# Graph attention and a mixture of experts on one core: the V projection moved into the batch before, four of 32 transposed copies moved to VectorE, and the second K projection moved to slot 7

## The reference, cut to what matters

```
x: (16, 512, 256) float32,  adj: (16, 512, 512) int32,  8 heads of 32

def gnn(x, adj):                       # x is the layer-normed input
    q, k, v = x @ Wq.T, x @ Wk.T, x @ Wv.T        # split in 8 heads
    s    = where(adj != 0, q @ k^T / sqrt(32), -inf)
    attn = softmax(s)
    c    = attn @ v
    gate = sigmoid(concat(c, x) @ Wg.T + bg)
    return gate * x + (1 - gate) * c

x = x + gnn(layernorm(x), adj)
x = x + ffn(layernorm(x))              # 8 experts, top 2 of them per token, and a shared expert
```

## Time and profile before

| what | value |
|---|---|
| median of 3 runs | 1810.76 us (1809.15 to 1811.35) |
| the profiled execution, its own time | 1823.27 us |
| its span, first to last instruction | 1820.5 us |
| mean granted TensorE clock | 0.987 |
| busy share: PE, DVE, ACT, POOL | 95%, 70%, 61%, 35% |
| passes of the attention | 16 passes of 32 slots, from 25.8 to 867 us |

### The profile page before, as it was taken

The page is one execution under the profiler, slowest core; times in us unless marked ns, Lnnn a source line. Parts: engine busy times, 40 slices in busy tenths (PEclk is TensorE's granted clock), DMA queues, the critical chain, the costliest instruction groups (busy, mean ns, idle before and its releaser), DMA issues. The chain is left out here.

```text
span 1820.5 us, 35931 instructions
## 1 busy us (share of the span) xinstructions
PE 1726.1 (95%) x12469; PEld 1456.1 (80%) x12469; DVE 1279.7 (70%) x3185; ACT 1102.4 (61%) x2509; POOL 643.7 (35%) x479
## 2 busy tenths in 40 slices
PE   5899999999999999999899999899999999999996
PEld 4677787777777777777688888789888989888986
DVE  5677877877777777777455554577778777777773
ACT  4888888988888888888434333234434343443442
POOL 0135544344554444454131000023344433444334
PEclk8999999999999999998999999999999999999999
DMA  5454565555555555554243344365565555565553
GB/s 150 127 158 132 159 174 162 169 153 173 142 151 174 163 164 165 161 156 124 84 137 105 104 152 140 128 202 133 165 168 163 155 160 139 163 174 163 141 142 38
DMA packets 140946, 269.19 MB, mean 148 GB/s; under 512 B 15072, under 2 KB 92256, under 8 KB 135776
## 3 DMA queue, kind: packets, MB, share of 16 engines
q1 hardware_dynamic: 113760, 230.45, 41.1%
q0 software_dynamic: 26592, 35.67, 9.7%
q10 hardware_dynamic: 416, 0.79, 0.2%
HBM read 141.99 MB, written 74.52 MB: 119 GB/s over the span
## 5 line engine op out<-in xcount | busy, mean ns | idle before, releaser
L849 DVE CUSTOM_DVE_ANT_0 pf<-bank,bias_q 128x512 f32<-128x512 f32 x512 | 349.1, 688 | 195.1 <-PE bank L493 179.6
L1202 POOL DMA_INDIRECT out_x<-yb,ix x142 | 247.7, 1745 | 567.7 <-ACT yb L1426 467.5
L1438 ACT ACTIVATE ah<-am 128x512 fp32r<-128x512 f32 (+1 forms) x220 | 133.1, 605 | 440.5 <-DVE am L1506 434.5
L622 ACT ACTIVATE pf<-pf,nmax 128x512 f32<-128x512 f32 x512 | 374.2, 731 | 32.8 <-DVE nmax L849 29.9
L1337 PE MATMUL bank<-xh,wh 128*128 128x512 f32 (+1 forms) x880 | 336.3, 382 | 0.9 <-ACT pt L610 0.9
L1338 PE MATMUL bank<-xl,wh 128*128 128x512 f32 (+1 forms) x880 | 335.7, 381 | 0.0
L1339 PE MATMUL bank<-xh,wl 128*128 128x512 f32 (+1 forms) x880 | 335.1, 381 | 0.0
L503 PE MATMUL bank<-ident,pf 128*128 128x128 f32 x2048 | 314.4, 276 | 21.0 <-ACT pt L610 15.8
L503 PEld LDWEIGHTS bank<-ident,pf 128*128 128x128 f32 x2048 | 252.4, 142 | 81.8 <-issue 34.6
L610 ACT ACTIVATE pt<-bank 128x512 f32<-128x512 f32 x512 | 306.9, 599 | 12.0 <-PE bank L503 10.0
L493 PE MATMUL bank<-stack 96*128 96x512 f32 x512 | 234.8, 459 | 27.3 <-DMA stack<-qk 23.6
(11 more groups left out here) (209 smaller groups left out, 3073.6 us busy)
## 6 DMA issues: line engine op xcount, KB each, us to landing
raw<-in_w_all SPq DMA_DIRECT2D x39, 1536.0 KB, 7.1
stack<-qk SPq DMA_DIRECT2D x378, 128.0 KB, 2.4
xb<-xg_dram SPq DMA_DIRECT2D x32, 520.0 KB
adj_i<-in_adj SPq DMA_DIRECT2D x32, 512.0 KB, 4.7
xn<-in_x SPq DMA_DIRECT2D x16, 512.0 KB, 6.4
xn_dram<-xn SPq DMA_DIRECT2D x16, 512.0 KB
xp<-in_x SPq DMA_DIRECT2D x16, 512.0 KB, 6.6
xnp<-xn_dram SPq DMA_DIRECT2D x16, 512.0 KB, 7.8
```

What stands on the lines that cost most here:

```text
L622: act.activation(pf[i][:, :], pf[i][:, :], ACT.Exp, bias=nmax[:, i:i + 1], scale=-1.0, accum_out=den[:, g, tq, j:j + 1]).then_inc(p_exp, 1)
L849: dve.tensor_tensor_reduce(pf[r][:, :], S[p % 2][:, :], bias_q[1 - par][:, tq, :], -SCALE, -3.0 * MASKED, ALU.add, ALU.min, nmax[:, r:r + ...
L1202: pool.indirect_dma_start(out=out, out_offset=bass.IndirectOffsetOnAxis(ap=ix[n % RING][:, i:i + 1], axis=0), in_=yb[s][:, i, :], in_offse ...
L1438: act.activation(ah[s][:, m, 0:cols], am[m % 2][:, 0:cols], ACT.Copy).then_inc(s_ah, 1)
```

## The change

It does four things. V0 and V1 leave slots 6 to 9 and are made one pass earlier, in slots 26, 27, 29 and 30 of pass `b` for batch `b+1`, from the same transposed input that K0 reads; V gets a second buffer (`v0`, `v1`, by the parity of the batch), so that PV of the running batch still reads its own. X0 and X1 go from slots 29 and 30 to 27 and 28. K1 goes from slots 4 and 5 to 7 and 8. Of the 32 copies of P^T of a batch, those of tiles 6, 10, 24 and 30 are made by DVE instead of ACT; each stands behind the mask of slot 10, 14, 28 and (of the next pass) 2, and has a semaphore of its own (`t_freed`). SP sends the 12 pieces of heads 0 to 3 in another order, heads 0 and 1 first.

```
-UNIT_AT = {"L0": 0, "M0": 1, "Q1": 2, "K1": 4, "V0": 6, "V1": 8, "C0": 10, "C1": 11, "R0": 12, "Z0": 14, "Z1": 15, "Z2": 16,
-           "Z3": 17, "P0": 18, "P1": 19, "Q0": 22, "K0": 24, "X0": 29, "X1": 30}
+UNIT_AT = {"L0": 0, "M0": 1, "Q1": 2, "K1": 7, "C0": 10, "C1": 11, "R0": 12, "Z0": 14, "Z1": 15, "Z2": 16, "Z3": 17,
+           "P0": 18, "P1": 19, "Q0": 22, "K0": 24, "V0": 26, "X0": 27, "X1": 28, "V1": 29}
+TURNED_BY_DVE = (6, 10, 24, 30)
...
-        v = sb("v", [P, NT, NH, DK])
+        v0 = sb("v0", [P, NT, NH, DK])
...
-                        for r in range(GRP):
+                        for r in (0, 1):
                             send_head(sp, r, range(2))
                         sp.wait_ge(g_free, unit(b, "K0") + 1)
-                        for r in range(GRP):
+                        for r in (0, 1):
                             send_head(sp, r, range(2, 3))
+                        for r in (2, 3):
+                            send_head(sp, r)
...
                     for kf in range(KF):
-                        last = split(o[:, D * piece:D * piece + D], xt_h[1 - s][:, kf, P * i:P * i + P],
-                                     xt_l[1 - s][:, kf, P * i:P * i + P], wqkv_h[:, kf, 2 * D:],
+                        pe.wait_ge(g_free, unit(b, f"P{kf}") + 1)
+                        last = split(o[:, D * piece:D * piece + D], xt_h[s][:, kf, P * i:P * i + P],
+                                     xt_l[s][:, kf, P * i:P * i + P], wqkv_h[:, kf, 2 * D:],
...
-                        pe.wait_ge(t_free, n - 1)
+                        if (n - 2) % POS in TURNED_BY_DVE:
+                            pe.wait_ge(t_freed, by_dve(n - 1))
+                        else:
+                            pe.wait_ge(t_free, n - 1 - by_dve(n - 1))
...
-                if was:
+                if was and ep not in TURNED_BY_DVE:
...
+                eb, ep, was = behind(b, p, EVAC, att)
+                if was and ep in TURNED_BY_DVE:
+
+                    n = eb * POS + ep
+                    dve.wait_ge(t_full, n + 1)
+                    if not isinstance(eb, int) or eb > 0 or ep >= 16:
+                        dve.wait_ge(pv, eb * 4 + ep // TB_ - 1)
+                        dve.nop().then_inc(s_held_dve, 1)
+                    g, r, j, tq = tile_of(ep)
+                    dve.tensor_copy(pt[r][:, j, :, P * (tq % 2):P * (tq % 2) + P],
+                                    T[ep % 2][:, :].rearrange("p (k q) -> p k q", q=P)).then_inc(t_freed, 1)
```

More of the change, by code:

```diff
@@ L41 @@
 Attention = namedtuple("Attention", "sync tensor scalar vector pool unit RT s_done t_free t_full pv s_rt g_full g_free "
-                                    "s_st s_ref s_xnst")
+                                    "s_st s_ref s_xnst t_freed by_dve")
 Experts = namedtuple("Experts", "sync tensor scalar vector pool count")
@@ L176, in attention_phase @@
         ea = sb("ea", [P, NT])
+        v1 = sb("v1", [P, NT, NH, DK])
+        v = [v0, v1]
         s_w = sem("s_w")
@@ L197, in attention_phase @@
         t_free = sem("t_free")
+        t_freed = sem("t_freed")
         pv = sem("pv")
@@ L257, in has @@
             kind = name[0]
-            return (late(b) if kind in "RLM" else att if kind == "V" or name in ("Q1", "K1") else
+            return (late(b) if kind in "RLM" else att if name in ("Q1", "K1") else
                     post if kind in "CZX" else pre)
@@ L290, in tile_of, with by_dve @@
             return p // 16, p // 8 % 2, p % GRP, 2 * (p // 8 % 2) + p % 8 // GRP
+        def by_dve(n):
+            return n // POS * len(TURNED_BY_DVE) + sum(t < n % POS for t in TURNED_BY_DVE)
         def f32(t):
@@ L517, in at @@
                     if ep == 0:
-                        pe.wait_ge(g_free, unit(eb, "V1") + 1)
+                        pe.wait_ge(g_free, unit(eb - 1, "V1") + 1)
                     if r == 0 and not (isinstance(eb, int) and eb == 0 and g == 0):
                         pe.wait_ge(s_norm, eb * 2 + g)
-                    pe.wait_ge(t_free, eb * POS + ep + TB_)
+                    n = eb * POS + ep + TB_
+                    pe.wait_ge(t_free, n - by_dve(n))
+                    if by_dve(n) > by_dve(n - TB_):
+                        pe.wait_ge(t_freed, by_dve(n))
                     for kt in range(NT):
@@ L524, in at @@
                             last = pe.matmul(C[DK * j:DK * j + DK, HALF * r:HALF * r + HALF],
-                                             v[:, kt, GRP * g + j, :], pt[r][:, j, kt, :],
+                                             v[eb % 2][:, kt, GRP * g + j, :], pt[r][:, j, kt, :],
                                              start=kt == 0, stop=kt == NT - 1)
@@ L720, in low @@
                         dve.nop().then_inc(s_held_dve, 1)
-                    dve.tensor_copy(v[:, 2 * k:2 * k + 2, :, :].rearrange("p i h d -> p (i h) d"),
+                    dve.tensor_copy(v[par][:, 2 * k:2 * k + 2, :, :].rearrange("p i h d -> p (i h) d"),
                                     o[:, :].rearrange("p (j d) -> p j d", d=DK)).then_inc(g_free, 1)
@@ L984, in attention_phase @@
         return Attention(sync, tensor, scalar, vector, pool, unit, RT, s_done, t_free, t_full, pv, s_rt, g_full, g_free,
-                         s_st, s_ref, s_xnst)
+                         s_st, s_ref, s_xnst, t_freed, by_dve)
 def ffn_phase(nc, sems, held, banks, att, w_dram, xt2_dram, x1_dram, xg_dram, out, ident, msum, s_scat, nb, slots,
@@ L1347, in gate_up @@
                     pe.wait_ge(att.s_done, nb * slots)
-                    pe.wait_ge(att.t_free, nb * slots)
+                    pe.wait_ge(att.t_free, nb * slots - att.by_dve(nb * slots))
+                    pe.wait_ge(att.t_freed, att.by_dve(nb * slots))
                 k0 = n * MT + m
@@ L1657, in prepare @@
                     if part == 0:
-                        dve.wait_ge(att.g_full, att.unit(nb - 1, "V1") + 1)
+                        dve.wait_ge(att.g_full, att.unit(nb - 1, "K1") + 1)
                         dve.wait_ge(att.s_xnst, nb * 16)
```

## The result

The changed kernel takes 1863.15 us in the median (1860.03 to 1866.09, 4 runs) where the kernel before, run beside it, takes 1810.12 (1809.15 to 1811.35, 4 runs): a ratio of 1.0291, with a 95% interval of 1.0279 to 1.0303. The forecast was slower, 1829, with eight in ten for 1803 to 1848: the sign is right and the size is not. Its profiled execution took 1866.09 us, its span is 1864.3, at a mean granted clock of 0.976.

What follows compares the result with a forecast made beforehand. PE itself was taken to bound slots 0 to 14, with waits for ACT and DMA later. Passes 1 to 14 at 14 x (2.6 - 1.8) = +11, pass 0 -1, clock +8: +18 on 1810.8, so 1829; eight in ten 1803 to 1848.

Steps and rivals of the forecast that it cites:

- the wait for xn2 in slot 27: PE reaches X0 before POOL's xn2 is ready and waits 2.2 us in each of passes 1 to 14.
- the copy in slot 14: DVE's copy behind its mask is ready late for the next turn: 0.1 us a pass, leaving a front gain of 1.8.
- pass 0: First pass, without X or Z; its V is made while PE waits for the first heads: -1 us.
- pass 15: Last pass, makes no V: 1.8 us gained in front against about the same wait, 0 in sum.
- the 12.5 us taken off between a profiled execution and the median: Profiled execution stood 12.5 us above the median; forecast 1841 profiled was carried over as 1810.8 + 18 = 1829.
- the price of the half clock: Behind X0's wait, half the passes run 3.4 us at half clock: 1.2 us each, seven times, 8 us; bounds 0 and 24.
- The prediction's own signs: Main step wrong if X0 waits under 1 us or pass under 52.0; second if first 14 slots under 19 or over 20.8.
- V out of 6-9, slots 0 to 13: Taking V's 3.20 us of PE work out of the front gains 1.9 us a pass, bounds 1.0 to 3.2.
- end of pass, slots 18 to 31: X0's wait and V's work at the pass's end start the next pass 2.6 us later, without the clock.
- Four copies on DVE: PE's turns lose up to 0.5 us in slot 10, 0.3 in 2, 0.1 in 14; only the last cost extra.
- K1 in slot 7: adj: adj's second half lands later, DVE stands up to 3 us in slots 16 and 17; costed at 0, up to 0.7.
- the upper one: Rival, chance 0.20: nearly all passes lose the clock, or adj comes late as well; 1842 to 1849 us.

Runs made afterwards that it cites:

- e2: Changed kernel with eight extra 128x512 products on PE ahead of X0 in passes 1 to 14, filling the wait: 1849.3 us, ratio 1.0207.
- e9: The kernel before, unchanged, run again for a second trace: 1813.84 us, trace span 1812.1.
- e12: The changed kernel, unchanged, run again for a second trace: 1860.96 us, trace span 1859.2.
- e7: Changed kernel with V in slots 26 to 29, X in 29 and 30, no copies on DVE, K1 in slot 4 in pass 0 only: 1820.21 us, ratio 0.9983.
- e8: Kernel before with V alone moved to slots 26 to 29 (second buffer); X in 29 and 30, K1 in 4, no DVE copies: 1829.88 us, ratio 1.0039.
- e5: Changed kernel with the four copies of P^T back on ACT: 1862.84 us, ratio 1.0217.
- e10: Changed kernel with X back in slots 29 and 30 and DVE's four copies ahead of its mask instead of behind it: 1812.24 us, ratio 1.0013.
- e4: Changed kernel with K1 back in slots 4 and 5: 1870.82 us, ratio 1.0312.
- f2: e10 with K1 in slot 4 in pass 0 alone: 1807.21 us, ratio 0.9976.
- e1: Changed kernel with X0 and X1 back in slots 29 and 30, V in 26 to 29: 1828.92 us, ratio 1.0091.

## Why the prediction was right or wrong, step by step

The sum said +18 and the medians say +53. The main mechanism, the wait for xn2 in slot 27, was right. What failed are terms that the sum put at nearly nothing or at a fixed value: the copy in slot 14 (0.1 us a pass; the slots took 0.67 more), pass 0 (-1; +4.7), pass 15 (0; +4.1), the 12.5 us taken off between a profiled execution and the median (2.9 for the changed kernel), and the price of the half clock (1.2 us a pass; 1.75).

The prediction's own signs did not catch this: X0 waits more than 1 us, the pass is longer than 52.0, and the first 14 slots take 20.11, between 19 and 20.8. They watched the steady passes, and most of the error lay outside them. By its own steps, in us (14 passes where a pass is meant):

```
step                                 forecast   measured   from
V out of 6-9, slots 0 to 13          14 x -1.9   14 x -1.57   table
copy in slot 14, slots 14 to 17      14 x +0.1   14 x +0.67   table
end of pass, slots 18 to 31,
  without the clock                  14 x +2.6   14 x +2.17   e2 against before: 23.91 - 21.74
clock behind X0                         +8         +14        after against e2
pass 0                                  -1          +4.7      traces
pass 15                                  0          +4.1      traces
start, and behind the attention          0          +7.0      traces (e9 to e12: +1.4)
carried from the trace to the median     0         +10        43 between profiled executions, 53 between medians
```

The measured terms add up to 57.6; slots are medians here, and the means of before's passes are 0.36 us above them, which takes 5 off again. The +7.0 stays open: what follows the attention takes 950.7 to 962.9 us over all the traces, without a link to the change, and in the second pair it differs by 0.8.

**V out of the front: right in kind, 0.3 us short a pass.** The gain of 1.57 is inside the bounds of 1.0 to 3.2. But less than half of it is V's. Slot 0 put aside, since X's place changes it in e7 and e8, slots 1 to 13 take 20.23 us before, 19.53 with V moved (e8: 0.70 gained), 18.41 with K1 in slot 7 as well (e7; 18.40 in e5: 1.12 more), and 18.68 in the changed kernel, where the copies take 0.28 back. The forecast gave all of the gain to V; most of PE's free time in slots 5 to 9 came to something only when K1 was laid into it.

**Four copies on DVE: the step that failed in slot 14.** The forecast let the copy be "ready 1.9 us after the slot's start", with DVE at hand when S is done. In slot 14 DVE comes a microsecond late from the statistics, and it was ready 3.4 us after it. The forecast had 0.1 us for it, the row shows 0.43 of plain wait, the slot 0.63. Slots 3 and 11 lost 0.48 and 0.42 where up to 0.3 and 0.5 were named, so the places were right. e10 shows that it is the place behind the mask and not the work: with the copy ahead of the mask all three are gone and ACT's relief is left. Net over slots 0 to 17 the change gains 0.9 us a pass, not 1.8; 12.6 us.

**K1 in slot 7: adj.** In passes 1 to 14 costed at 0 and measured at 0: DVE waits for adj in slot 16 by 0.85 to 3.35 us, about the forecast's "up to 3", and the Z units cover it. The view of the line says 34.9 us in 17 waits (two of them ahead of pass 0), against 5.2 in 6 before:

```profile
L702 DVE TENSOR_SCALAR bias_q<-adj_i x32: 687/693/973, 10.5 to 818.9; 128x1024 bf16<-128x1024 int32 x32
...
  DMA adj_i<-in_adj: 34.9, 17
```

The step that failed is pass 0. The forecast gave it -1, saying itself that it "has no X and no Z": with no Z units there is nothing that hides a late adj. 2.46 us of DVE's wait stood there in the trace of before already. e4 gives pass 0 6.5 us back with K1 in slot 4, e10 to f2 6.6. The net is 4.7, since slot 31 of that pass falls from 3.21 to 0.59 us and no longer waits for head 0.

**The wait in slot 27: right.** 2.2 forecast, 2.00 to 2.16 measured, put down to POOL's xn2, with PE reaching X0 45.0 us into the pass and xn2 ready at 46.9. Its price without the clock, 2.6, was somewhat high against the first trace of before (2.17) and right against e9's (2.64). e1 takes it away and with it 2.0% of the time. That it "does not shrink by the gain in front" held: fronts of 19.8 to 21.6 us (e5, after, e4) gave waits of 2.0 to 2.2.

**The clock: right in kind, 6 us short.** Half of the passes was a guess between two rows, and it was borne out: 8 of 14, and 7, 9 and 5 in the traces of e12, e5 and e4. The price of one was forecast at 1.2 us and is 14 / 8 = 1.75; nothing of the 1.7 that PE loses was taken up by DVE and ACT.

**Pass 15: not seen.** Its xn2 is late for another reason (timelines of POOL and PE):

```profile
888.28 8.17 POOL L1008 TENSOR_SCALAR xn<-x,mv,rstd 128x256 f32<-128x256 f32 x4 [0.24 <-POOL rstd L1002]
```

```profile
896.60 1.09 PE L421 MATMUL bank<-ident,xn 128*128 128x128 f32 x4 [5.03 <-POOL xn L1008]
```

It took 8.17 us in the trace of before too, at 857.16, and nobody waited for it in slot 29. The clock adds to it: it was at half from 853.3 to 863.5 us in pass 15 before and is from 885.2 to 902.3 now. It fell there ahead of the X0 wait, behind a wait of 1.96 us for DVE's mask in slot 23. The forecast took pass 15 as one like the others.

**The carrying over: wrong by 10 us.** The 12.5 us between the profiled execution of before and its median were taken as the profiler's own. They were not: the changed kernel's are 2.9, and e9's trace is 8.4 us shorter. Some 11 of the 12 us are 0.8 us a pass in slots 18 to 26, which the kernel before shows in one trace and not in another (last section). Half of V in slot 26 was said to be covered by the wait in slot 27. It is, in the first trace. Against e9 these slots grow by 0.8 us, the whole of the half unit.

**The rival that it came nearest to** is the upper one, nearly all passes losing the clock or adj late as well, 1842 to 1849 (its 38 leaves out the -1 of pass 0; with it, 1848). It came out above that, by what none of the cases had: pass 0, pass 15, slot 15 and the carrying over.

## What to carry to other kernels

Cost the first and the last turn of a pipelined loop by themselves: a late transfer or a late producer that the middle turns hide has nothing to hide behind there, and here that was nearly 10 us that the sum didn't have. When an engine takes over a copy, ask where its queue stands at that moment, not how long the copy is: the same four copies made the kernel before 1.4% slower behind the mask, and ahead of it slots 0 to 17 took 0.5 us a pass less than with no such copies. An operation that waits for another engine's late result belongs at the end of the work that doesn't, and a wait of two microseconds on PE may be paid nearly twice, once as idle time and once in the clock.
